# A state-space scan loop on one core: the order of a key/value round inside each step, its sums of squares in two groups, and the next layer's weights loaded in ten pieces during the loop

## Time and profile before

| | |
|---|---|
| median of three runs | 1465.5 us |
| the profiled execution, and its span | 1465.39 us, 1463.5 us |
| TensorE busy in the span | 1312.8 us (90%) |
| VectorE busy | 1022.4 us (70%) |
| ScalarE busy | 707.2 us (48%) |
| GpSimd busy | 270.1 us (18%) |
| mean granted TensorE clock | 0.947 of full |
| products of step 0 start, those of step 31 | 41.52 us, 180.59 us |
| last add of layer 1 ends | 192.24 us |

### The profile page before, as it was taken

How to read it: one execution, slowest core, us unless ns; L and a number is a source line. 1 busy time by engine, 2 the same in 40 slices (tenths; PEclk the granted TensorE clock), 3 DMA queues, 4 the chain that set the end, 5 groups by cost and what they waited for, 6 DMA issues and landing times.

```text
span 1463.5 us, 20903 instructions
## 1 busy us (share of the span) xinstructions
PE 1312.8 (90%) x6697; PEld 917.8 (63%) x6697; DVE 1022.4 (70%) x2266; ACT 707.2 (48%) x1824; POOL 270.1 (18%) x256
## 2 busy tenths in 40 slices
PE   7788869989998667999999799995999999989998
PEld 4354445555333244676667589984888888765555
DVE  7888777889896787887788623235666666667665
ACT  5777613443775665555554212223666666633111
POOL 0666520000000002222121173121111111201000
PEclk8899979999999769999999799997999999979999
DMA  6476640015430200000004198855222222102230
GB/s 224 153 221 214 218 180 0 1 23 94 70 56 2 83 0 1 1 37 1 37 1 131 33 348 320 305 192 180 99 72 72 72 72 72 36 1 48 79 93 29
DMA packets 82434, 141.53 MB, mean 97 GB/s; under 512 B 45493, under 2 KB 56958, under 8 KB 77008
## 3 DMA queue, kind: packets, MB, share of 16 engines
q1 hardware_dynamic: 80480, 136.28, 29.6%
q0 software_dynamic: 1872, 4.22, 0.8%
HBM read 105.06 MB, written 26.37 MB: 90 GB/s over the span
## 4 chain that ended last, share of the span: by engine, by line
PE 67%; DVE 10%; ACT 3%; issue 2%; DMA 2%; POOL 1%; SPq 0%; DVEq 0%; ACTq 0%; POOLq 0%
PE psum L3295 5%; PE psum L2496 5%; PE psum L2068 4%; PE psum L958 4%; PE psum L2792 4%; PE psum L2844 4%; PE psum L2822 4%; PE psum L2110 4%; PE psum L2857 3%; PE psum L3305 3%; PE psum L2507 2%; DVE roomB L1624 2%; PE psum L2100 2%; PE psum L2800 2%; PE psum L992 2%
## 5 line engine op out<-in xcount | busy, mean ns | idle before, releaser
L2914 ACT ACTIVATE roomA<-psum,roomA 128x256 f32<-128x256 f32 x128 | 70.9, 559 | 87.4 <-DVE roomA L2981 86.9
L2165 ACT ACTIVATE roomA<-psum,roomA 128x128 f32<-128x128 f32 (+1 forms) x128 | 53.2, 426 | 84.4 <-DVE roomA L2240 84.2
L1624 DVE TENSOR_REDUCE roomB<-psum 128x2 f32<-128x512 f32 x128 | 81.4, 686 | 8.8 <-PE psum L1463 8.2
L2031 POOL TENSOR_TENSOR roomA<-roomA 128x512 f32<-128x512 f32 x40 | 50.8, 1270 | 177.0 <-DVE roomA L2233 177.0
L875 POOL TENSOR_TENSOR roomA<-roomA 128x1024 f32<-128x1024 f32 (+1 forms) x32 | 74.5, 2328 | 48.3 <-PE psum L596 31.4
L530 PE MATMUL psum<-roomB,own 128*128 128x256 f32 x256 | 69.6, 402 | 15.2 <-ACT roomB L632 14.7
L2644 DVE SCALAR_TENSOR_TENSOR roomA<-roomA,psum 128x512 f32<-128x512 f32 x23 | 15.9, 690 | 95.5 <-ACT roomA L2543 89.4
L2068 PE MATMUL psum<-own,roomB 128*128 128x512 f32 x160 | 75.0, 594 | 3.4 <-DVE roomA L2232 2.1
L530 PEld LDWEIGHTS psum<-roomB,own 128*128 128x128 f32 x256 | 48.1, 196 | 46.1 <-ACT roomB L632 26.0
L3295 PE MATMUL psum<-roomA,roomB 128*112 128x512 f32 (+1 forms) x168 | 74.8, 593 | 0.3 <-DVE roomA L3523 0.3
L796 DVE TENSOR_TENSOR_SCAN roomA<-roomA,psum 128x512 f32<-128x512 f32 x64 | 74.4, 1204 | 0.0
(11 more groups left out here) (520 smaller groups left out, 3325.3 us busy)
## 6 DMA issues: line engine op xcount, KB each, us to landing
roomB<-m_w_dram SPq DMA_DIRECT2D x12, 1536.0 KB
roomA<-m_w_dram SPq DMA_DIRECT2D x11, 1536.0 KB
a_kv_ready<-roomB SPq DMA_DIRECT2D x32, 512.0 KB, 3.6
roomA<-m_c_rows SPq DMA_DIRECT2D x32, 512.0 KB, 4.8
roomA<-a_kv_ready SPq DMA_DIRECT2D x8, 1024.0 KB, 4.8
roomA<-a_kv_ready SPq DMA_DIRECT2D x16, 512.0 KB, 4.3
roomB<-a_w_dram SPq DMA_DIRECT2D x4, 1280.0 KB, 6.0
roomB<-f_w_dram SPq DMA_DIRECT2D x8, 624.0 KB, 4.0
```

Source lines behind the costliest of these rows:

```text
L1624: dve.tensor_reduce(maxneg[:, hp // 8, :, m, hp % 8], g.bank(m).rearrange("p (q k) -> p q k", k=S), AX.X, ALU.max, negate=True).then_inc(s ...
```

## The change

1. **TensorE's order in step k** becomes `spread(k+1)`, second half of round k-1, `add(k-1)`, first half of round k. So a round's halves stand in neighbouring steps, and `add` stands between the second half of one round and the first half of the next. `add(31)` moves ahead of `back(0)`.
2. **The squares in two groups of four**: in step k ScalarE does `decay(k+1)`, the second group of round k-2, the copy of round k-1, the first group of round k-1. The semaphore `m_k_squared` counts groups (32 in all), and VectorE waits for it ahead of the four adds to `x` instead of behind them. The buffer `k_sq` moves to another place in SBUF; an unused buffer goes.
3. **The stores** of a round are issued one step later (`k - 2 in round_at`).
4. **The weights of layer 2** are no longer loaded by layer 2. Ten DMAs (the router's 8 KB, six of 384 KB for `w_up`, three of 384 KB for `w_down`) are issued by SyncE in steps 14 to 23, one in each, behind the step's row and store.

```diff
-            if k - 1 in round_at:
-                keep(round_at[k - 1])
+            if k - 2 in round_at:
+                keep(round_at[k - 2])
+            if 0 <= k - WEIGHTS_AT < g.f0_parts:
+                g.f0_part(sp, k - WEIGHTS_AT)
...
-            if k in round_at:
-                kv_round(round_at[k], range(0, 2))
+            if k - 1 in round_at:
+                kv_round(round_at[k - 1], range(2, 4))
             if k:
                 add(k - 1)
             if k in round_at:
-                kv_round(round_at[k], range(2, 4))
-        pe.wait_ge(s["m_kv_copied"], 32)
+                kv_round(round_at[k], range(0, 2))
+        add(STEPS - 1)
+        pe.wait_ge(s["m_kv_copied"], ROUNDS)
         pe.wait_ge(s["m_products"], 2 * STEPS)
         back(0)
-        add(STEPS - 1)
         back(1)
...
+            if k - 2 in round_at and kind_of[round_at[k - 2]] == 0:
+                squares(round_at[k - 2], 1)
             if k - 1 in round_at:
-                r = round_at[k - 1]
-                kv_out(r)
-                if kind_of[r] == 0:
-                    squares(r)
+                kv_out(round_at[k - 1])
+                if kind_of[round_at[k - 1]] == 0:
+                    squares(round_at[k - 1], 0)
...
+        dve.wait_ge(s["m_k_squared"], 32)
         for b in range(4):
             dve.wait_ge(s["m_back"], b + 1)
             xs = g.X[:, 2 * b:2 * b + 2, :].rearrange("p i d -> p (i d)")
             dve.tensor_tensor(xs, xs, g.bank(4 + b), ALU.add).then_inc(s["layer_done"], 1)
-        dve.wait_ge(s["m_k_squared"], 16)
...
+    pieces = [(w_gate, d["f0_gate"])]
+    pieces += [(w_up[:, kt, e:e + 3], d["f0_up"][:, kt, e:e + 3]) for kt in range(KD) for e in range(0, E, 3)]
+    pieces += [(w_down[:, e:e + 3], d["f0_down"][:, e:e + 3]) for e in range(0, E, 3)]
+    g.f0_parts = len(pieces)
+    g.f0_part = lambda sp, i: sp.dma_start(*pieces[i]).then_inc(s["f0_weights"], 16)
 
     def sync(sp):
-        sp.dma_start(w_gate, d["f0_gate"]).then_inc(s["f0_weights"], 16)
         keys.sync(sp)
-        for kt in range(KD):
-            sp.dma_start(w_up[:, kt], d["f0_up"][:, kt]).then_inc(s["f0_weights"], 16)
-        sp.dma_start(w_down, d["f0_down"]).then_inc(s["f0_weights"], 16)
...
-        pe.wait_ge(s["f0_weights"], 64)
+        pe.wait_ge(s["f0_weights"], 16 * g.f0_parts)
```

More of the change, by code:

```diff
@@ L444, in mamba @@
     ones = rb.take(2 * NS, dt=BF16, rows=96)
-    k_sq, k_tmp = rb.take(8, P), rb.take(3, 16 * NT)
-    rb.at = 10200
+    assert rb.at <= 1200
+    rb.at = 9176
+    k_sq = rb.take(8, P)
     w_kv = rb.take(16, 2 * P)
@@ L455, in mamba @@
     first_free = {0: ("m_xpad", 2), 2: ("m_xpad", 4)}
-    IN_LOOP = 32 - AHEAD
+    ROUNDS, WEIGHTS_AT = 32, 14
+    IN_LOOP = ROUNDS - AHEAD
     round_at = {1 + i * 29 // IN_LOOP: AHEAD + i for i in range(IN_LOOP)}
@@ L461, in mamba @@
     assert len(keys) == len(values)
-    kind_of = [int(r in values) for r in range(32)]
-    place_of = [(values if kind_of[r] else keys).index(r) for r in range(32)]
+    kind_of = [int(r in values) for r in range(ROUNDS)]
+    place_of = [(values if kind_of[r] else keys).index(r) for r in range(ROUNDS)]
     xpad = ra.take(E2, B, S + TAPS - 1)
@@ L632, in kv_out, with squares @@
             act.copy(staged[:, r % 4].rearrange("p q (i c) -> p q i c", i=4), src).then_inc(s["m_kv_copied"], 1)
-        def squares(r):
+        def squares(r, q):
             pair, half = divmod(place_of[r], 2)
@@ L637, in squares @@
             if place_of[r]:
[L638 to L642, removed]
+                act.wait_ge(s["m_k_squared"], 2 * place_of[r] - 1 + q)
+            for i in range(4):
+                ins = act.activation(k_sq[:, 4 * q + i, :], staged[:, r % 4, q, i * P:(i + 1) * P], ACT.Square, scale=float(P) ** -0.5,
+                                     accum_out=g.k_ss[:, 2 * pair + q, 4 * half + i:4 * half + i + 1])
             ins.then_inc(s["m_k_squared"], 1)
```

## The result

The changed kernel takes 1448.14 us, the median of four runs (1447.00 to 1450.64), against 1464.93 (1463.31 to 1468.17) for the kernel before on the same chip: a ratio of 0.9885, with a 95% interval of 0.9862 to 0.9908. The prediction was 1447.8. The profiled execution took 1447.14 us with a span of 1445.4.

A forecast was written before the change was run, and what follows sets the result against it. TensorE was taken to set the loop's pace, with 3.87 us of work and 0.94 of waiting a step. Loop 16.2, start 0, end 0.9, layer 2's start 1.0, loads -0.5: 17.6 off 1465.4 gives 1447.8 us, range 1444 to 1452.

The forecast's parts named there:

- the missing 0.94: TensorE in loop steps: 4.81 us a step against 3.87 of work; the rest is waiting for ScalarE's copy.
- ScalarE's lateness: Copies in the loop: late copies after rounds of keys make TensorE wait, 2.7 us in all.
- Rival 1: ScalarE sets the loop's pace: each of 16 rounds of keys costs 0.63 us, 7.4 more, 1455 us; chance 0.15.
- Steps 19 to 31: Last stretch of the loop, products 19 to 31: 49.77 us before, 44.3 forecast, a gain of 5.5.
- The split of the squares is what leaves that room: ScalarE in the loop: with the squares split, decays behind late copies still end before their scans, 0.2 us to spare.
- Rival 5: Another wait in the loop, such as the decay, takes the 0.94 every step: no change, about 1463.5 us; chance 0.03.
- The start of the loop: First steps, `add(0)` ahead of the first half-round, TensorE partly at its lower clock: taken as 0 us.
- rival 3: Start of the loop: the lower clock lasts one step longer, 3.9 us of work counts twice, 1452 us; chance 0.05.
- The end: Behind the loop: `add(31)` ahead of the eight transposes starts 0.87 us earlier, a gain of 0.9.
- Layer 2's start: Layer 2's router matmuls no longer wait for the last weight load, only for the last copy: a gain of 1.0 us.
- The loads: Ten weight loads in steps 14 to 23: extra DMA traffic, mostly taken up by slack, costs 0.5 us.
- Rivals 2 and 4: DMA queue in the loop: 300 GB/s or less, 1451 us, chance 0.13; or 216 GB/s at most, 1480 us, chance 0.04.

The follow-up runs named there:

- whole squares: The changed kernel with all eight squares of a round behind its copy, as before: 1447.94 us, ratio 0.9888.
- weights late: The changed kernel with the ten loads taken out of the loop and layer 2 loading its weights itself again: 1448.93 us, ratio 0.9886.
- four loads: The changed kernel with layer 2's weights in four loads (8 KB, three of 1152 KB) instead of ten: 1449.35 us, ratio 0.9881.
- free steps 7, 13, 24: The changed kernel with squares in groups of two and no round at steps 7, 13, 24, 30 and 31: 1445.82 us, ratio 0.9865.
- extra stores: The changed kernel with a 384 KB store to a scratch tensor behind each of the ten loads: 1447.34 us, ratio 0.9884.

## Why the prediction was right

- **What bounds the kernel, and the missing 0.94**: right. The order alone turned 4.81 a step into 3.88 or a little over; no other wait took its place. The signs named came: products 4 to 10 are 3.88 to 4.41 apart, those of 20 to 22 3.42, VectorE's idle time is 7.8, and the DMA share with the loads 0.88 to 1.01. Only TensorE's wait for the copy, 0.8 in the list, was to be 2 to 3: part of the 2.2 sits in later starts and longer durations, as the 0.09 and 0.10 at 66.11, which the list doesn't count. And the router starts 0.14 behind the copy, where 0.1 was given.
- **ScalarE's lateness**, 2.7 in the loop: 2.2 by the steps (0.18 + 0.19 + 0.53 + 0.19, then 0.18 for products 11 to 17 and 0.90 for 19 to 31), each at a place that the forecast names. This is the term that was sized too large. A second round of keys costs 0.53, not 0.63: copy to copy is 4.44 and not 4.5. Rival 1 fell: after values the copies catch up.
- **Steps 19 to 31**: 44.3 predicted, 44.33 measured, with two small errors against each other. TensorE's falling behind, less its lead, was counted 3.2 - 1.1 = 2.1 and is 2.4 (0.07 and five times 0.46); the copies were counted 1.15 and are 0.90.
- **"The split of the squares is what leaves that room"**: right on the room, but the room is worth little. One scan, at 88.73, waits 0.29 for its decay even with the split. Without it nine scans wait, and that mostly uses up idle time that VectorE has anyway. The split is worth 0.14 in the loop and 0.53 at the end. Rival 5 rested on the same error: the whole squares make the decay late, and the loop still keeps 16.14 of the 16.28.
- **The start of the loop**: products 0 to 3 take 12.14, before 12.12, as the 0 taken has it. In part that is the luck of this execution: they take 12.41 in the changed kernel's second one, and 13.40 to 13.41 in three variants (weights late, four loads, free steps 7, 13, 24), whose granted clock was still 0.50 to 0.52 over 50 to 54 us, against 0.94 in the changed kernel's second execution. So the condition of rival 3 does come about, at 1.3 us and not 3.9.
- **The end**: 0.9 predicted, 0.87 measured, and 0.87 lost again with the transposes first.
- **Layer 2's start**: the mechanism is right, the router starts 0.14 behind the copy. The term was 1.0 and measured 0.65 against the profile before, since norm and transposes took 0.27 more in this execution. Undone in the changed kernel it is 2.0: there the load came 2.04 behind the copy instead of 1.06. Why the late loads then land later isn't settled.
- **The loads**: 0.5 taken, 0 measured. Rivals 2 and 4 fell with the 353 GB/s of the changed kernel and the 402 of the extra stores. The rate of single slices, not the mean of a window in which the queue had pauses, was the one to go by. The Trainium skill, DMA: Bandwidth & Descriptors, under Specifications, has 358 GB/s; the run with extra stores exceeds it by 12%. The Trainium skill, HBM Reference, under Specifications (TRN2), says that a core streaming alone gets well above its share of 358, and with that this trace agrees. The Trainium skill's rule to make DMAs 1 MiB or more (DMA: Bandwidth & Descriptors, under Bandwidth) bound nothing here: pieces of 384 KB between transfers of 512 KB made up the 402 GB/s, and three loads of 1152 KB left the loop as it was.
- **The sum**: 17.6 predicted. Its terms measured 16.28 - 0.02 + 0.87 + 0.65 + 0 = 17.78. The profiles differ by 18.25 us, the medians by 16.8. Up to the router's start the changed one is 19.84 ahead: 16.28 in the loop, 0.87 and 0.65, and 2.06 ahead of product 0, where no instruction changed (products 0 to 3 give 0.02 back). Over the 14 profiled executions product 0 starts anywhere from 38.70 to 41.52. That part is spread and not the change. Behind the router the lead of one instruction over its like in the kernel before moves between 18.4 and 24.7 us. Two executions of the changed kernel itself come 6.0 us apart there, and are 0.2 apart at the end, so this is spread too. That the total lies within 0.4 us of the forecast is partly luck; that the loop does is not.

## What to carry to other kernels

When two engines hand a buffer back and forth, add up the pacing engine's work in a step apart from its waits, and look for independent work to fill the hand-over (here 1.06 + 1.06 us from the start of the second half, of which that half's own matmuls fill 0.86) and put it ahead of the next first half. Cost a new wait on an engine that is not the pacing one against the idle time that it has in that step already, step by step: where it sets the pace itself, the wait counts in full. After a gain that makes TensorE idle longer in one place, look at the granted clock behind that place, and leave a free step there in which the lead can be won back.

## What the runs showed of the hardware

- At the same place of the program TensorE's granted clock stayed at 1.00 behind an idle time of 1.11 to 1.13 us in eight traces (the changed kernel twice, and six of its variants). Behind 1.83 to 1.84 us it fell to 0.51 for some 3 us in three kernels and stayed at 1.00 in one. What makes the difference there is not shown.
- A group of matmuls ahead of the loop (eight of 512 columns, unchanged) took 6.20 us in the profile before, from 26.9 us on, and 4.24 in the one after, from 26.7 on. The granted clock fell to its lower level at 27.9 us in the first and at 29.7 in the second. In all 14 profiles product 0 starts 8.4 to 9.0 us behind the end of this group, and so moves by up to 2.8 us with it. The Trainium skill, TensorE: Matmul & The Clock Gate, Part 1, says that the number of slow matmuls differs from run to run of one kernel; these traces agree.
- Stores, broadcast rows and weight loads together ran at 402 GB/s over 19 us, at a DMA share of 1.03.
- A ScalarE instruction can start before the one ahead has ended: a decay of 1.13 us is followed by a square 1.03 us after its start. Behind a copy it is not so: one of 1.01 us is followed by a square 1.05 us after its start.
